# Backward-scan loads of a two-layer kernel, issued some slots sooner

## The reference

```python
x1 = _layernorm(tok, g1, b1)             # tok: group-normed x, as tokens
x = x1 @ W_in_x.T                        # 192 -> 384 channels
z = x2 @ W_in_z.T
y_f = _branch(x, ...)                    # forward in time
y_b = _branch(x[:, ::-1, :], ...)[:, ::-1, :]
y = (y_f + y_b) * silu(z)
out = y @ W_out.T + b_out
# _branch: a causal convolution with 4 taps per channel, silu, a projection to
# dt (12), B (16) and C (16), then for each of 384 channels and 16 states
h = h * exp(dt * A) + (dt * x) * B_t
y_t = sum_n h * C_t,  + x * D
```

## Time and profile before

| | |
|---|---|
| median of 3 runs | 20159.46 us (20150.19 to 20165.52) |
| the profiled execution | 20123.45 us, its span 20121.7 us |
| busy: TensorE, VectorE, ScalarE, GpSimd | 87%, 86%, 70%, 84% |
| mean granted TensorE clock | 0.938 |
| DMA | 108 GB/s mean, 1905 MB read, 246 MB written |

### The profile page before, as it was taken

How to read it: one execution, slowest core, us unless ns; L and a number is a source line. 1 busy time by engine, 2 the same in 40 slices (tenths; PEclk the granted TensorE clock), 3 DMA queues, 4 the chain that set the end, 5 groups by cost and what they waited for, 6 DMA issues and landing times. The chain is left out here.

```text
span 20121.7 us, 179901 instructions
## 1 busy us (share of the span) xinstructions
PE 17468.9 (87%) x43392; PEld 7664.0 (38%) x43392; DVE 17219.6 (86%) x13583; ACT 13992.6 (70%) x35077; POOL 16825.7 (84%) x10932
## 2 busy tenths in 40 slices
PE   7888988889888898888988889888898888988889
PEld 3433434334343343433434334343343433434334
DVE  7988979889798897988979789797897978979789
ACT  6767767577676776767767577675776767767677
POOL 6978969789697896978969799696996979969699
PEclk9989989899899998989989899898998989989899
DMA  2313323133231332313323133231332313323233
GB/s 85 135 65 129 137 76 134 65 129 137 76 134 66 128 137 76 134 65 128 137 77 133 66 128 136 77 133 65 129 136 76 134 65 135 130 77 135 73 132 124
DMA packets 528855, 2178.88 MB, mean 108 GB/s; under 512 B 96328, under 2 KB 243424, under 8 KB 527648
## 3 DMA queue, kind: packets, MB, share of 16 engines
q1 hardware_dynamic: 527648, 2165.99, 29.8%
HBM read 1905.47 MB, written 245.63 MB: 107 GB/s over the span
## 5 line engine op out<-in xcount | busy, mean ns | idle before, releaser
L1032 DVE TENSOR_TENSOR_SCAN arena<-ps,arena 128x897 f32<-128x897 f32 x5376 | 10963.7, 2066 | 993.9 <-ACT arena L1188 761.6
L1240 POOL TENSOR_TENSOR arena<-arena 128x896 f32<-128x896 f32 x5376 | 9427.4, 1769 | 901.5 <-PE ps L962 619.8
L962 PE MATMUL ps<-arena,ident 128*128 128x448 f32 x21504 | 8979.4, 556 | 879.6 <-POOL arena L1240 876.2
L1172 ACT ACTIVATE ps<-arena,A 128x448 f32<-128x448 f32 x10752 | 6412.1, 632 | 1749.0 <-DVE arena L1032 1705.3
L962 PEld LDWEIGHTS ps<-arena,ident 128*128 128x128 f32 x21504 | 4049.3, 193 | 5473.3 <-issue 3690.3
L1232 POOL TENSOR_TENSOR arena<-arena 128x896 f32<-128x896 f32 x2688 | 4773.6, 1776 | 0.2 <-DMA arena<-bc_rows 0.2
L1021 DVE TENSOR_TENSOR arena<-ps,arena 128x896 f32<-128x896 f32 x2688 | 2868.0, 1067 | 30.4 <-ACT ps L1134 30.4
L919 PE MATMUL ps<-arena,diag 128*128 128x448 f32 x5376 | 2178.4, 549 | 154.0 <-issue 141.8
L919 PEld LDWEIGHTS ps<-arena,diag 128*128 128x128 f32 x5376 | 1014.8, 192 | 1233.9 <-issue 1097.4
L1094 ACT ACTIVATE arena<-ps,vece 128x448 f32<-128x448 f32 x672 | 423.3, 630 | 948.5 <-PE ps L919 948.5
L1188 ACT ACTIVATE arena<-arena 128x2 f32<-128x2 f32 x5376 | 1045.8, 195 | 50.9 <-DVE arena L1032 50.9
(11 more groups left out here) (160 smaller groups left out, 19406.9 us busy)
## 6 DMA issues: line engine op xcount, KB each, us to landing
arena<-bc_rows SPq DMA_DIRECT2D x1792, 896.0 KB, 5.4
x_projected<-arena SPq DMA_DIRECT2D x112, 672.0 KB, 3.5
y_forward<-arena SPq DMA_DIRECT2D x112, 672.0 KB, 3.9
arena<-x_projected SPq DMA_DIRECT2D x112, 672.0 KB, 7.7
arena<-y_forward SPq DMA_DIRECT2D x112, 672.0 KB, 4.1
x<-in_x SPq DMA_DIRECT2D x119, 336.0 KB, 3.6
x_normed<-arena SPq DMA_DIRECT2D x112, 336.0 KB, 2.8
arena<-x_normed SPq DMA_DIRECT2D x112, 336.0 KB, 4.2
```

The source lines that it names most:

```text
L962: m = e.matmul(y, ident[:, :], pr[:, q % NPR, a * T:a * T + T], start=False, stop=p == NP - 1 and a == 1)
L1032: e.tensor_tensor_scan(rev(hh[:, q % NH, 0:W2], s), rev(decays(q)[:, 0:W2], s), rev(bb[:, q % NB, 0:W2], s), car[:, k, n:n + 1] if i % NC ...
L1172: e.activation(two(decays(q))[:, a, :], dt[:, r % NDT, :], ACT.Exp, scale=Am[s][:, k, 2 * p + a:2 * p + a + 1]).then_inc(c_ex, 1)
L1240: e.tensor_tensor(pr[:, q % NPR, :].rearrange("p (a b) -> p a b", a=2), two(hh[:, q % NH, :]), cr[:, 2 * p:2 * p + 2, :], ALU.mult).then_i ...
```

## The change

Four due slots on SyncE's list change, and no other line. The load of the projected x of a backward visit goes from t to t-8, that of the normed x from t+15 to t+9, that of the backward taps from 150 to 133 (24*5+13), and that of the forward taps from 314 to 301 (24*12+13). What each entry waits for stays as it is.

```diff
         else:
-            sp += [(t, "xl", i, 0), (t + 15, "nl", i, 0)]
+            sp += [(t - 8, "xl", i, 0), (t + 9, "nl", i, 0)]
             for e, v in enumerate((1.3, 8.7, 10.7)):
                 conv(i, e, t + v)
...
-    sp += [(PER * (NC - 1) + 6, "dg", 1, 0), (PER * (NI - 1) + 2, "dg", 0, 0)]
+    sp += [(PER * (NC - 2) + 13, "dg", 1, 0), (PER * (NI - 2) + 13, "dg", 0, 0)]
```

## The result

The changed kernel takes 19981.9 us (median of 6 runs, 19976.3 to 19987.8). The kernel before, run beside it, now has 20147.5 (6 runs, the three first shown among them): the ratio is 0.9918, with a 95% interval of 0.9905 to 0.9931, and the difference 166 us. The forecast was 140 us from 20159, that is 20019, with a range from 19985: the direction is right, and the time is 3 us under the range. From profile to profile the difference is only 20121.7 - 19986.0 = 135.7 us of span. The two sizes lie 30 us apart, so the experiments had two questions: which of the moved loads did it, and how large the gain is.

What follows compares the result with a forecast made beforehand. GpSimd was taken to bound the second layer, stalled once an image by TensorE waiting for late backward taps. Removing that stall gives 140 us, the other loads 0: 20159.5 - 140 = 20019 us, range 19985 to 20085.

Steps and rivals of the forecast that it cites:

- What bounds, and what TensorE waits for: Second layer: GpSimd bounds, VectorE near second; TensorE's 8.82 us wait before visit 7's convolution is for the backward taps.
- Rival B: At visit 7's convolution the wait is not for the taps: idle time stays at 145 us, time 20159; chance 0.04.
- a remainder of 0.9 us: Image 2, visit 7: taps land at 1970.4, some 0.9 us ahead of the first convolution matmul.
- the 2.5 us that taps alone were to leave: With only the backward taps moved, visit 7's projected x still holds TensorE 2.5 us of its 8.82.
- The lengths of the stretches: Second layer, store to store: forward stretches 70.8 us in every image, the one preparing visit 7 76.9 to 79.6.
- The term of the gap, 140 us: GpSimd's idle time at the first backward visit, once an image, goes: 16 x (9.08 - 0.3) = 140 us gained.
- Rival C: Behind visit 7's convolution, some 4 of 8.8 us stay as VectorE's slack runs out: time 20082; chance 0.07.
- Projected x, normed x, forward taps at 0 us: Projected x of visits 8 to 13 0 us (ends 0 and 9 gained); normed x and forward taps 0 us.
- Rival A: Backward stretches of visits 8 to 12 all go to 71.7 us by the clock: 32 us lost, 20051; chance 0.09.
- Rival D: Store of visit 6's B and C rows late behind two moved loads: slower, 20270 at 30 us late; chance 0.03.
- The step that failed: Last of the sum: the profile's 140 us taken from the median of the runs, 20159.5 - 140 = 20019.

Runs made afterwards that it cites:

- the second pair of profiles: Kernel before and changed kernel, each run again with no edit for a second profile: 20125.2 us (ratio 0.9998) and 19978.0 us (ratio 0.9928).

## Why the prediction was right in its mechanism and wrong in its time

*What bounds, and what TensorE waits for.* Right. "Issue" was the backward taps: moved alone they give the whole gain, moved by a third of the way 103 of 145 us, and nothing else does that. Rival B (another operand) is out. The landing of this one load shows the same. In image 2 of before it took 7.8 us from its issue at 1963.4, where the prediction took the median of 7.0 and had a remainder of 0.9 us:

```profile
L1257 SPq DMA_DIRECT2D diag<-taps x1: 432/432/432, 1963.4 to 1963.4; - x1
DMA to landing us min/median/max: 7.8/7.8/7.8
```

That is 1971.2, and TensorE starts at 1971.26. In all 16 images of each profile in which this wait is put down to "issue", the convolution starts 0.09 us after its taps have landed. The 0.9 us was also a term of the 2.5 us that taps alone were to leave. That 2.46 came is in part luck: no such 0.9 us exists, but the second load of projected x, issued 0.6 us behind the first, was left out and makes up for it.

*The lengths of the stretches.* The forward stretches are 70.8 us but for the first of an image, which the prediction passed over: it is 60.3. Nothing was worked out from it.

*The term of the gap, 140 us.* Right within 5%. The stretches got 146.9 us shorter, 9.2 an image where 9.08 - 0.3 = 8.8 was forecast; by the second pair of profiles it is 139.0. Nothing took the gap's place there, and the stretch came out at 68.8 us, shorter than the 69.5 that the forward neighbours gave. Rival C, a new wait of 4 us, didn't come.

*Projected x, normed x, forward taps at 0 us.* Right for the whole change: beside the moved taps they bring at most the 4 us between 19982 and 19978, less than the runs' spread. Read alone on the old kernel, the zero for the projected x was wrong, since it gives 48 us there, and the loads of visits 8 to 13 by themselves 30, where their ends were 0 and 9 us. The runs don't show why.

*Rival A, the clock.* It came, beside the forecast and not in its place. The stretches of visits 8 to 12 settled near 71.5 us in all images of the first profile, and cost 17.9 us, of the 32 that it allowed. At the same place of the visit, with nearly the same work, TensorE had a full clock in the kernel before and a fall of about 4 us in the changed one. Four us each, the changed kernel first, then the kernel before:

```profile
2075.00:2079.00 4.00, 3.31 (x9) 1.18 (x7) 3.76 (x5) 2.05 (x6) 4.00 (x4) 0.98 0.60 236
2079.00:2083.00 4.00, 4.00 (x7) 1.99 (x8) 3.69 (x3) 4.00 (x12) 3.08 (x2) 0.59 0.86 330
```

```profile
2084.70:2088.70 4.00, 3.28 (x9) 1.19 (x8) 3.74 (x5) 2.05 (x7) 4.00 (x4) 1.00 0.63 215
2088.70:2092.70 4.00, 4.00 (x11) 2.05 (x12) 3.72 (x3) 4.00 (x13) 4.00 (x3) 1.00 0.82 341
```

TensorE was 83% and 82% busy in the first rows, and then had 7 matmul records in 4 us at 0.59 against 11 at 1.00. What decides between the two is not shown.

*Rival D, late rows.* It didn't come: the taps landed in 4.1 to 4.5 us and the projected x in 5.7 at the median, well ahead of the store.

*The step that failed* is the last of the sum: "the median of the runs lies 36 us above the profiled one, for which I have no row, and I take the same 140 us from it". The three runs shown were high ones. The kernel before scatters by 86 us (20082 to 20168 in 29 runs), its median is 20127 in those 29 and in 21 others, and the profiled execution is 3 us from that; in 6 and 9 further runs, the three first among the 6, the median is 20148 and 20144. From 20127 the same 140 us give 19987, 5 us from what was measured, and a range moved with it would have held the result.

The range had a fault of its own. It was worked out as a gain of 105 to 185 us, which from 20159.5 is 19974.5 to 20054.5, and this holds 19982; put down was 19985 to 20085, which leaves the larger gains out.

That 140 from 20127 meets the time within 5 us is luck in part. The gap brought 139 to 147 us and the clock took 17 to 18 back, and the means of the two profiles of each kernel are only 125 us apart, while the medians differ by 149 or more. Of the two profiled executions of before, 20123.5 is near the median and 20092.5 among the fastest; what the slower ones spend more isn't shown.

Why before scatters so much isn't shown either. Its gap on GpSimd is 8.0 to 10.7 us, by how late the taps land and by how long the clock stays low behind it, and the last visit and the first layer differ by 26 us between its two profiles. The changed kernel scatters by 18 us over 11 runs, but the gap alone is not the reason. With it in place ten of eleven runs with the projected x moved lie within 11 us, and without it the kernel with the convolution a slot sooner has its four runs spread over 43 us.

## What to carry to other kernels

A load that only waits for a free moment in a hand-ordered DMA queue is late by what stands ahead of it, not by its due time: look at the issue times of all loads that one instruction waits for, and move the last to land. An idle time of an engine that feeds the bound costs what exceeds the bound's own backlog: here 2.46 us of TensorE's waiting cost GpSimd 0.41 us, a backlog of some 2 us. What the low clock adds behind a long wait comes on top: 8.8 us cost 8.2, with 1.6 us for the slower convolution (4.74 us against 3.17), and 4.3 cost 3.9 with 1.8. Where a time is forecast, set it against as many runs of the old kernel as there are, and let the range hold their scatter too.

## What the runs showed that was not expected

Moving the projected x alone, with the gap in place, made the kernel 48 us faster, and each half of that move 30 to 34. With the taps moved neither was seen. One slot for one of the three convolutions of each backward visit was worth about 96 us, two thirds of the whole change, and was found by looking at the largest waits that the removed gap left behind.
